# Rotary passes of an attention on Trainium2, split between two steps: two table products in the odd step, the third product and the sum in the even step behind it

## The chip, the cores and the metric

The kernel runs on one core of one Trainium2 chip. The metric is the time of one execution in device microseconds (us). TensorE, VectorE, ScalarE, GpSimd and SyncE are called PE, DVE, ACT, POOL and SP, as in the profile. Each of them works through its own instruction stream in order, and they meet at semaphores.

## The reference, cut to what matters

A two-layer block over 8 sequences of 512 tokens with width 128, all in 32-bit floats. The first layer is a causal attention with two query heads and one shared key and value, gated by a mixture of experts (8 experts, 2 per token). The second layer is a recurrent block with a gated feed-forward part. The change touches only the rotary embedding of queries and keys in the first layer:

```python
k = apply_rope(x @ Wk.T)
v = x @ Wv.T
q = jnp.einsum('btd,hkd->bhtk', x, Wq)
q = apply_rope(q)
scores = jnp.einsum('bhtk,bsk->bhts', q, k) * scale
...
# apply_rope: xr = x.reshape(..., d // 2, 2)
out = jnp.stack([xr[..., 0] * cos - xr[..., 1] * sin, xr[..., 1] * cos + xr[..., 0] * sin], axis=-1)
```

## The kernel before, in words

The program is written out per engine, in four stages. First all 4096 tokens are normalised and turned, and the router's logits are made. Then comes the attention of sequences ("batches") 0 to 6, while POOL scatters the tokens by expert into DRAM (lines 474 to 503). Then 71 tiles of 128 slots go through their experts. Last is the attention of batch 7 and the recurrent layer. The order of the work within a stage is fixed by the order in which the Python code issues instructions on each engine. There is no planner.

The attention of one batch is eight steps, k = 0 to 7. A step is one tile of 128 queries of one head, and its width is the causal part of the keys: 512 columns at k = 0 and 2, 128 at 1 and 3, 384 at 4 and 6, 256 at 5 and 7 (STEPS, line 45). So the even steps are the wide ones, and the odd steps the narrow ones. In step k the engines issue, in this order:

- PE (`attend`, L733): `scores(k)` (L687 the products, L689 the mask added on top), which needs the exponential of step k-2, since the two share a bank. In odd steps `project` for the next batch comes behind it (parts 0, 1, 2 are the two queries and the key, L668, at k = 1, 3, 5; part 3 is the value times output product, L671, at k = 7). Then `turn(k-1)` (L701, four or fewer transposes), which needs exponential k-1, and `weigh(k-2)` (L720), which needs the copy of turn k-2.
- DVE (`attend`, L1154): `row_max(k)` (L1147), which needs the scores of k, and `denominator(k-1)` (L1152, a reciprocal), which needs exponential k-1. In steps 5, 6, 1 and 2 one `combine` follows (L1140, 128x128). In steps 1, 3 and 5 one pass `rope` for the next batch follows (L1116).
- ACT (`attend`, L1539): a `head0` copy in some steps, `exponent(k)` (L1513), which needs the row maximum of k, and `turned(k-1)` (L1522). At the batch's end are the two `values` copies (L1535, L1536).

One `rope` pass is four DVE instructions on 512 columns: RT1 = bank times cosines (L1125, all partitions), the two halves of RT2 = bank times sines with the partition halves crossed (L1126, L1127, 64 partitions each), and the sum RT1 + RT2 into QT (L1130). L1127 is the last to read the PSUM bank and counts `proj_free`. A wait on that count stands before L1130 (L1129). L1130 counts `qk_done`.

Parts 0 and 2 of a batch use PSUM bank 0, part 1 uses bank 1, part 3 uses both. So PE waits at L664 before it projects: parts 0 and 1 for the `values` copies of the batch before, part 2 for L1127 of part 0, and part 3 for L1127 of part 2. `scores(0)` of a batch waits for its third `qk_done` (L682).

Batch 0 is special on DVE: step 0 has the second half of the router's top-2 choice, step 1 the slot numbers, and step 5, behind the rope pass, `experts()` (L1109 to L1113, which lets SP start to load expert weights). Batch 7 has no rope pass.

Of the kernel before, what the change touches and what calls it, by code (L numbers as in the profile page):

```python
# [26 lines left out]
P = 128  # L27
# [50 lines left out]
def build(nc, t, out):  # L78
    ctx = ExitStack()
    with ctx:  # L80
# [164 lines left out]
        B = [ctx.enter_context(nc.psum_tensor(f"bank{i}", [P, 512], F32)) for i in range(8)]  # L245
# [760 lines left out]
        def _(dve):  # L1006
# [60 lines left out]
            def choose_both(half):  # L1067

                n = NT // 2
                tiles = slice(half * n, (half + 1) * n)  # L1070
                logits = by_expert(B[6 + half][:, 0:n * E])
                dve.wait_ge(a_lg, NSEQ // 2 * (half + 1))
                choose(0, logits, half)
                link(dve.scalar_tensor_tensor(out=LG2[:, tiles, :], in0=by_expert(OH[:, 0, :])[:, tiles, :],
                                              scalar=BELOW, in1=logits, op0=ALU.mult, op1=ALU.add))
                choose(1, LG2[:, tiles, :], half)
                cols = slice(half * n * E, (half + 1) * n * E)
                dve.tensor_tensor(SH[:, tiles, :], logits, TOP[:, 0, tiles, None].broadcast_to([P, n, E]), ALU.subtract)
                dve.tensor_tensor(DIF[:, tiles], TOP[:, 1, tiles], TOP[:, 0, tiles], ALU.subtract).then_inc(r_sh, 1)
                dve.tensor_tensor(MB[:, cols], OH[:, 0, cols], OH[:, 1, cols], ALU.add).then_inc(r_m, 1)  # L1080

            def slots():

                dve.wait_ge(r_cnt_out, 1)
                link(dve.tensor_reduce(SUMT, TOTS[:, :, 1:], AX.X, ALU.add))
                link(dve.tensor_scalar(REM, SUMT, (P - 1) / 2, ULP_IS_P, ALU.add, ALU.add))
                link(dve.tensor_scalar(TCN, REM, ULP_IS_P, None, ALU.subtract))
                dve.wait_ge(prep, 3)
                link(dve.tensor_tensor_scan(CTL, ONES, TCN, 0.0, ALU.mult, ALU.add))
                link(dve.tensor_tensor(TOTS[:, :, 0], CTL, TCN, ALU.subtract))  # L1090
                link(dve.tensor_tensor_scan(EXB.rearrange("p e n -> p (e n)"),
                                            CST[:, C_RESET:C_RESET + E * (NT + 1)],
                                            TOTS.rearrange("p e n -> p (e n)"), 0.0, ALU.mult, ALU.add))
                link(dve.tensor_tensor(POS, LOWER, EXB[:, :, 0:NT].rearrange("p e n -> p n e"), ALU.add))
                link(dve.tensor_tensor(PIC, POS.rearrange("p n e -> p (n e)")[:, None, :].broadcast_to([P, 2, NT * E]),
                                       OH, ALU.mult))
                link(dve.tensor_reduce(SLF.rearrange("p k n -> p (k n)"),
                                       PIC.rearrange("p k (n e) -> p (k n) e", e=E), AX.X, ALU.add))
                dve.tensor_copy(SLOT[:], SLF).then_inc(r_slot, 1)

            def gates():

                dve.wait_ge(r_exp, 1)
                link(dve.tensor_reduce(SUME, SH, AX.X, ALU.add))
                dve.reciprocal(GATE[0], SUME).then_inc(r_gate0, 1)

            def experts():

                link(dve.tensor_tensor(CM2, CTL[:, None, :].broadcast_to([P, SLOT_TILES, E]),  # L1109
                                       CST[:, C_TILE:C_TILE + SLOT_TILES, None].broadcast_to([P, SLOT_TILES, E]),  # L1110
                                       ALU.is_le))
                link(dve.tensor_reduce(TEF, CM2, AX.X, ALU.add))
                dve.tensor_scalar(TEXP[:], TEF, float(E - 1), None, ALU.min).then_inc(r_texp, 1)  # L1113


            def rope(b, u, part):  # L1116

                tab = 2 if part == 2 else 0
                m = 3 * b + part
                dve.wait_ge(proj_full, 4 * b + (part + 1))  # L1120
                if not (isinstance(m, int) and m == 0):
                    dve.wait_ge(qk_done, m)
                bank = B[part % 2]
                half = P // 2
                dve.tensor_tensor(RT1, bank[:], ROPE[:, tab, :], ALU.mult)  # L1125
                dve.tensor_tensor(RT2[0:half], bank[half:P, :], ROPE[half:P, tab + 1, :], ALU.mult)  # L1126
                dve.tensor_tensor(RT2[half:P], bank[0:half, :], ROPE[0:half, tab + 1, :], ALU.mult  # L1127
                                  ).then_inc(proj_free, 1)
                dve.wait_ge(proj_free, 4 * b + (part + 1))  # L1129
                dve.tensor_tensor(QT[u][part], RT1, RT2, ALU.add).then_inc(qk_done, 1)  # L1130

            def combine(b, c):

                k = {0: 2, 1: 3, 2: 6, 3: 7}[c]
                i, _ = STEPS[k]
                dve.wait_ge(pv_done, NS * b + (k + 1))
                dve.wait_ge(rd_done, NS * b + (k + 1))
                dve.wait_ge(o0_done, TPS * b + (c + 1))
                reg = B[6 + k % 2][:, 0:P]
                dve.scalar_tensor_tensor(out=SA[:, bass.ds(b * TPS + i, 1), :].rearrange("p a d -> p (a d)"), in0=reg,  # L1140
                                         scalar=RD[:, k:k + 1], in1=O0[c], op0=ALU.mult, op1=ALU.add
                                         ).then_inc(o_done, 1)

            def row_max(b, k):
                i, _ = STEPS[k]
                dve.wait_ge(s_full, NS * b + (k + 1))
                dve.tensor_reduce(NM[:, k:k + 1], B[2 + k % 2][:, 0:(i + 1) * P], AX.X, ALU.max,  # L1147
                                  negate=True).then_inc(max_done, 1)

            def denominator(b, k):  # L1150
                dve.wait_ge(exp_done, NS * b + (k + 1))
                dve.reciprocal(RD[:, k:k + 1], DEN[:, k:k + 1]).then_inc(rd_done, 1)  # L1152

            def attend(b, u, first=False, last=False):  # L1154
                for k in range(NS):
                    row_max(b, k)
                    if not (first and k == 0):
                        denominator(b if k else b - 1, (k - 1) % NS)
                    if isinstance(b, int) and b == 0:
                        if k == 0:  # L1160
                            choose_both(1)
                        if k == 1:
                            gates()
                            slots()
                    if k in (5, 6):
                        combine(b, k - 5)
                    if k in (1, 2) and not first:
                        combine(b - 1, k + 1)
                    if k in (1, 3, 5) and not last:
                        rope(b + 1, 1 - u, (k - 1) // 2)  # L1170
                    if isinstance(b, int) and b == 0 and k == 5:
                        experts()
                    if last:
                        if k == 6:
                            d_early_gate(0)
                            d_first_product()
                        if k == 7:
                            d_early_gate(1)
# [7 lines left out]
            dve.wait_ge(vo_done, 1)  # L1186
            dve.tensor_copy(CVO[:].rearrange("p h d -> p (h d)"), B[2][:, 0:2 * P]).then_inc(cvo_done, 1)
            rope(0, 0, 0)
            rope(0, 0, 1)
            choose_both(0)  # L1190
            rope(0, 0, 2)
            attend(0, 0, first=True)
            with dve.Fori(0, NB // 2) as i:
                attend(i * 2 + 1, 1)
                attend(i * 2 + 2, 0)
# [59 lines left out]
            def d_early_gate(b):  # L1255

                dve.wait_ge(d_th, b + 1)
                y = Y0[:, tiles(b), :]
                dve.scalar_tensor_tensor(out=y, in0=SIL[:, b, :].rearrange("p (i d) -> p i d", d=P), scalar=1.0, in1=y,
                                         op0=ALU.add, op1=ALU.mult).then_inc(d_g0, 1)  # L1260

            def d_first_product():
                dve.wait_ge(d_g0, 1)
                dve.tensor_tensor(Y0[:, 0:TPS, :], Y0[:, 0:TPS, :], SA[:, 0:TPS, :], ALU.mult).then_inc(d_sg, 1)
# [559 lines left out]
```

## Time and profile before

| | us |
|---|---|
| median of 3 runs | 585.35 (583.39 to 586.44) |
| the profiled execution, its own time | 584.18 |
| its span, first to last instruction | 582.3 |
| from scores(0) of batch 1 to the end of batch 6's eight steps | 65.48 to 169.1 |
| PE busy over the span | 546.8 |
| DVE busy over the span | 377.0 |
| ACT busy over the span | 276.7 |
| mean granted clock | 0.985 of full speed |

PE is the engine with most busy time, but its matmul ends are modelled, so a span without idle time in the record can still have short holes. The stages follow one another: the attention of batches 0 to 6 runs to about 172, the expert tiles to about 380, and the rest is batch 7 and the recurrent layer.

### The profile page before, as it was taken

To read this page: it belongs to the slowest core of one execution; us is meant where nothing else is said; L and a number is where in the kernel's file an instruction comes from. 1 tells how busy PE (TensorE), PEld (TensorE's weight loads), DVE (VectorE), ACT (ScalarE), POOL (GpSimd) and SP (SyncE) were. 2 spreads that over 40 slices of the span, in tenths; PEclk is the share of its full clock that TensorE was granted. 3 is DMA by queue.
4 is the path that set the end of the run, shared out by engine and by line. 5 is a ranking of instruction groups with operands and counts; after the bars stand their busy time and mean duration, and the time that the engine had idled before them with its cause. 6 is when DMAs were issued, how large, how long until landed. Compare 5 with 4: busy or idle time off the path is not lost. (4 is left out here: it accounts for less than half of the span.)

```text
span 582.3 us, 13385 instructions
## 1 busy us (share of the span) xinstructions
PE 546.8 (94%) x3327; PEld 401.7 (69%) x3328; DVE 377.0 (65%) x1071; ACT 276.7 (48%) x792; POOL 255.1 (44%) x385
## 2 busy tenths in 40 slices
PE   9957899999989999999999999997999999999984
PEld 4734666667669999999999999763554454454441
DVE  6968777877755655555555655566767766776521
ACT  4513465465555445555455455564553553454320
POOL 4203554665623444444444444442554654653210
PEclk9969999999999999999999999999999999999988
DMA  9920533211117887888787887190000000000000
GB/s 285 374 73 20 176 119 137 68 59 59 41 32 208 240 231 232 240 238 234 231 236 233 242 233 225 51 262 2 0 19 1 18 18 0 18 18 9 10 18 19
DMA packets 46107, 71.77 MB, mean 123 GB/s; under 512 B 6256, under 2 KB 32016, under 8 KB 45824
## 3 DMA queue, kind: packets, MB, share of 16 engines
q1 hardware_dynamic: 31536, 57.82, 33.4%
q0 software_dynamic: 4320, 8.92, 4.6%
q10 hardware_dynamic: 10224, 4.73, 2.9%
q8 instruction: 10, 0.16, 0.1%
q14 instruction: 17, 0.14, 0.1%
HBM read 54.14 MB, written 15.74 MB: 120 GB/s over the span
## 5 line engine op out<-in xcount | busy, mean ns | idle before, releaser
L1224 DVE SCALAR_TENSOR_TENSOR AR<-bank,B1T,AR 128x128 f32<-128x128 f32 x284 | 80.4, 344 | 75.6 <-ACT AR L1601 75.4
L521 POOL DMA_INDIRECT rows_y<-YO,DST x71 | 69.8, 982 | 96.7 <-DVE YO L1208 88.3
L1601 ACT ACTIVATE AR<-bank,BGT 128x128 f32<-128x128 f32 x284 | 81.0, 368 | 57.4 <-PE bank L810 57.4
L477 POOL DMA_INDIRECT slots_x<-XR,SLOT x64 | 63.2, 987 | 51.9 <-DMA slots_x<-XR,SLOT 32.0
L827 PE MATMUL bank<-W2E,AR 128*128 x568 | 75.1, 275 | 0.5 <-DVE AR L1224 0.5
L810 PE MATMUL bank<-AR,WGE 128*128 128x128 f32 x568 | 75.1, 275 | 0.3 <-ACT AR L1594 0.3
L818 PE MATMUL bank<-AR,WGE 128*128 128x128 f32 x568 | 75.0, 275 | 0.0
L827 PEld LDWEIGHTS bank<-W2E,AR 128*128 128x128 f32 x568 | 69.1, 192 | 0.7 <-issue 0.7
L810 PEld LDWEIGHTS bank<-AR,WGE 128*128 128x128 f32 x568 | 69.0, 192 | 0.6 <-issue 0.6
L818 PEld LDWEIGHTS bank<-AR,WGE 128*128 128x128 f32 x568 | 69.1, 192 | 0.0
L1513 ACT ACTIVATE AR<-bank,AR 128x512 f32<-128x512 f32 (+1 forms) x64 | 33.8, 529 | 64.9 <-DVE AR L1147 64.9
L720 PE MATMUL bank<-AR 128*128 128x128 f32 x320 | 46.7, 277 | 0.9 <-ACT AR L1531 0.9
L687 PE MATMUL bank<-AR 128*128 128x128 f32 (+3 forms) x128 | 46.2, 445 | 0.0
L1147 DVE TENSOR_REDUCE AR<-bank 128x1 f32<-128x512 f32 (+1 forms) x64 | 30.7, 483 | 23.7 <-PE bank L689 23.7
L1708 ACT ACTIVATE W1E<-bank 128x512 f32<-128x512 f32 x32 | 19.1, 597 | 56.7 <-PE bank L937 56.7
L701 PEld LDWEIGHTS bank<-CST,AR 128*128 128x128 f32 x160 | 17.6, 141 | 36.7 <-ACT AR L1513 27.9
L720 PEld LDWEIGHTS bank<-AR 128*128 128x128 f32 x320 | 40.8, 192 | 1.7 <-ACT AR L1522 1.6
L1381 DVE TENSOR_TENSOR W1E<-bank,W1E 128x512 f32<-128x512 f32 x32 | 22.1, 690 | 25.9 <-PE bank L943 24.7
L701 PE MATMUL bank<-CST,AR 128*128 128x128 f32 x160 | 29.6, 283 | 9.8 <-ACT AR L1513 9.8
L1594 ACT ACTIVATE AR<-bank 128x128 f32<-128x128 f32 x71 | 19.6, 277 | 39.6 <-PE bank L802 39.6
L948 PE MATMUL bank<-W1E,WDN 128*128 128x512 f32 x64 | 33.5, 615 | 1.5 <-DVE W1E L1381 1.3
L937 PE MATMUL bank<-WGE,WGT 128*128 128x512 f32 x64 | 33.7, 609 | 0.8 <-DVE WGE L1374 0.8
(190 smaller groups left out, 964.4 us busy)
## 6 DMA issues: line engine op xcount, KB each, us to landing
WGE<-in_wgu SPq DMA_DIRECT2D x71, 512.0 KB, 3.8
XG<-slots_x ACTq DMA_DIRECT2D x71, 65.0 KB, 3.3
slots_x<-W1E SPq DMA_DIRECT2D x7, 585.0 KB, 11.1
X<-in_x SPq DMA_DIRECT2D x8, 256.0 KB, 4.9
W2E<-in_w SPq DMA_DIRECT2D x1, 2048.0 KB, 8.7
XR<-rows_y SPq DMA_DIRECT2D x8, 256.0 KB, 4.8
XNT<-rows_y SPq DMA_DIRECT2D x8, 256.0 KB, 5.1
out<-X SPq DMA_DIRECT2D x8, 256.0 KB, 2.3
```

The costliest lines, as they stand in the source:

```text
L477: pool.indirect_dma_start(out=slots_x, out_offset=bass.IndirectOffsetOnAxis(ap=SLOT[:, k, n:n + 1], axis=0), in_=XR[:, n, :], in_offset=No ...
L521: pool.indirect_dma_start(out=rows_y, out_offset=bass.IndirectOffsetOnAxis(ap=DST[q][:, 0:1], axis=0), in_=YO[q % 2][:], in_offset=None).t ...
L687: pe.matmul(bank[:, 0:(i + 1) * P], QT[u][h][:, i * P:(i + 1) * P], QT[u][2][:, 0:(i + 1) * P], start=True, stop=False)
L701: mm = pe.transpose(B[4 + k % 2][:, j * P:(j + 1) * P], PR[k % 2][:, j * P:(j + 1) * P], ident)
L720: mm = pe.matmul(reg, PT[k % 2][:, j * P:(j + 1) * P], U[u][:, j, h * P:(h + 1) * P], start=(j == 0), stop=(j == i))
L810: mm = pe.matmul(B[1 + u][:, c * P:(c + 1) * P], WB[:, q, c * P:(c + 1) * P], XT[u], start=True, stop=True)
L818: mm = pe.matmul(B[3 + u][:, c * P:(c + 1) * P], WB[:, q, F + c * P:F + (c + 1) * P], XT[u], start=True, stop=True)
L827: mm = pe.matmul(B[5 + u][:, 0:P], HT[u][:, c, :], W2E[:, bass.ds(e, 1), c, :], start=(c == 0), stop=(c == FC - 1))
L937: pe.matmul(B[5 - 3 * (c % 2)][:], WGT[:, c * P:(c + 1) * P], H2, start=True, stop=True).then_inc(d_g, 1)
L1224: s = dve.scalar_tensor_tensor(out=HT[u][:, c, :], in0=B[3 + u][:, c * P:(c + 1) * P], scalar=B1T[:, bass.ds(e, 1), c], in1=ZB[u][:, c, :] ...
L1513: act.activation(PR[k % 2][:, 0:(i + 1) * P], B[2 + k % 2][:, 0:(i + 1) * P], ACT.Exp, bias=NM[:, k:k + 1], accum_out=DEN[:, k:k + 1]).the ...
L1601: act.activation(ZB[u][:, c, :], B[1 + u][:, c * P:(c + 1) * P], ACT.Gelu, bias=BGT[:, bass.ds(e, 1), c]).then_inc(c_gelu, 1)
```

## The change

`rope` becomes `rope_begin` and `rope_end`. In the attention's steps the first is called where `rope` was, in steps 1, 3 and 5, and the second at the same place of the next step, 2, 4 and 6. The three passes for batch 0, which run before the attention, call both parts in a row as before. No other line is touched. No instruction is added or removed.

```diff
             def rope(b, u, part):
 
+                rope_begin(b, part)
+                rope_end(b, u, part)
+
+            def rope_begin(b, part):
+
                 tab = 2 if part == 2 else 0
                 m = 3 * b + part
                 dve.wait_ge(proj_full, 4 * b + (part + 1))
...
                 half = P // 2
                 dve.tensor_tensor(RT1, bank[:], ROPE[:, tab, :], ALU.mult)
                 dve.tensor_tensor(RT2[0:half], bank[half:P, :], ROPE[half:P, tab + 1, :], ALU.mult)
+
+            def rope_end(b, u, part):
+
+                tab = 2 if part == 2 else 0
+                bank = B[part % 2]
+                half = P // 2
                 dve.tensor_tensor(RT2[half:P], bank[0:half, :], ROPE[0:half, tab + 1, :], ALU.mult
                                   ).then_inc(proj_free, 1)
                 dve.wait_ge(proj_free, 4 * b + (part + 1))
...
                     if k in (1, 2) and not first:
                         combine(b - 1, k + 1)
                     if k in (1, 3, 5) and not last:
-                        rope(b + 1, 1 - u, (k - 1) // 2)
+                        rope_begin(b + 1, (k - 1) // 2)
+                    if k in (2, 4, 6) and not last:
+                        rope_end(b + 1, 1 - u, (k - 2) // 2)
                     if isinstance(b, int) and b == 0 and k == 5:
                         experts()
```

So the first two products stay in the odd step, and the third product (which frees the bank) goes with the sum.

## Rows read from the trace of the kernel before

**Rows 1.** The page, part 1: busy us (share of the span) x instructions.

```profile
PE 546.8 (94%) x3327; PEld 401.7 (69%) x3328; DVE 377.0 (65%) x1071; ACT 276.7 (48%) x792; POOL 255.1 (44%) x385
```

**Rows 2.** Busy us by stretch: length, PE, PEld, DVE, ACT, POOL. Batches 5, 6; sum 1-6.

```profile
134.54:151.83 17.29, 16.56 (x99) 11.71 (x98) 13.59 (x32) 9.28 (x30) 10.22 (x13) 1.00 0.17 58
...
151.83:169.10 17.27, 16.61 (x101) 11.83 (x99) 13.71 (x32) 9.54 (x33) 8.08 (x10) 1.00 0.09 31
...
sum 103.62, PE 99.52 PEld 70.52 DVE 81.83 ACT 56.57 POOL 56.02; mean PE 16.59 PEld 11.75 DVE 13.64 ACT 9.43 POOL 9.34
```

**Rows 3.** Waits, 65.4 to 169.2: engine, line, whom for: us, times, longest.

```profile
DVE AR L1152 <- ACT AR L1513: 4.4, 14, 0.3
...
PE bank L701 <- ACT AR L1513: 4.1, 12, 0.5
...
PEld bank L671 <- DVE AR L1127: 0.5, 3, 0.2
```

**Rows 4.** Timeline of batch 5, PE: start us, us, engine, line ... [idle before <-releaser].

```profile
139.38 0.22 PE L689 MATMUL bank<-BFC 128*128 128x128 bf16 x1
...
142.31 0.66 PE L701 MATMUL bank<-CST,AR 128*128 128x128 f32 x4 [0.51 <-ACT AR L1513]
...
146.53 0.55 PE L701 MATMUL bank<-CST,AR 128*128 128x128 f32 x3 [0.22 <-ACT AR L1513]
...
149.23 1.99 PE L671 MATMUL bank<-CVO,AR 128*128 128x256 f32 x8
...
151.12 0.55 PE L701 MATMUL bank<-CST,AR 128*128 128x128 f32 x3
```

**Rows 5.** Timeline of batch 5, DVE.

```profile
138.73 0.69 DVE L1126 TENSOR_TENSOR AR<-bank,ROPE 64x512 f32<-64x512 f32 x1
...
140.76 0.68 DVE L1147 TENSOR_REDUCE AR<-bank 128x1 f32<-128x512 f32 x1
...
141.44 0.33 DVE L1140 SCALAR_TENSOR_TENSOR SA<-bank,AR 128x128 f32 x1
...
141.68 0.28 DVE L1147 TENSOR_REDUCE AR<-bank 128x1 f32<-128x128 f32 x1
...
142.29 0.16 DVE L1152 RECIPROCAL AR<-AR 128x1 f32<-128x1 f32 x1 [0.33 <-ACT AR L1513]
...
142.48 0.69 DVE L1125 TENSOR_TENSOR AR<-bank,ROPE 128x512 f32<-128x512 f32 x1
...
144.61 0.69 DVE L1130 TENSOR_TENSOR AR<-AR 128x512 f32<-128x512 f32 x1
...
145.22 0.55 DVE L1147 TENSOR_REDUCE AR<-bank 128x1 f32<-128x384 f32 x1
...
147.08 0.68 DVE L1125 TENSOR_TENSOR AR<-bank,ROPE 128x512 f32<-128x512 f32 x1
...
148.48 0.68 DVE L1127 TENSOR_TENSOR AR<-bank,ROPE 64x512 f32<-64x512 f32 x1
...
149.81 0.55 DVE L1147 TENSOR_REDUCE AR<-bank 128x1 f32<-128x384 f32 x1
...
150.35 0.33 DVE L1140 SCALAR_TENSOR_TENSOR SA<-bank,AR 128x128 f32 x1
```

**Rows 6.** Timeline of batch 0, steps 5 to 7, DVE and PE.

```profile
61.68 0.74 DVE L1109 TENSOR_TENSOR W1E<-W2E,CST 128x568 f32<-128x568 f32 x1
...
63.35 0.55 DVE L1147 TENSOR_REDUCE AR<-bank 128x1 f32<-128x384 f32 x1
...
64.66 0.55 PE L701 MATMUL bank<-CST,AR 128*128 128x128 f32 x3 [1.44 <-ACT AR L1513]
```

**Rows 7.** Timeline of batch 6: a sum beside POOL, and the scatter's end.

```profile
161.83 0.96 POOL L477 DMA_INDIRECT slots_x<-XR,SLOT  x1 [0.30 <-issue]
...
161.83 0.72 DVE L1130 TENSOR_TENSOR AR<-AR 128x512 f32<-128x512 f32 x1
...
164.24 0.46 POOL L507 TENSOR_TENSOR TAPW<-TAPW,CHN 128x128 f32<-128x128 f32 x1 [1.45 <-DMA slots_x<-XR,SLOT]
```

## The prediction

> **What bounds the kernel now.** The change acts only in the attention of batches 0 to 6, so I leave the page after its first part, which says that PE is busy 546.8 of 582.3 us [rows 1], and cut the attention into stretches, one a batch. Batches 1 to 6 take 103.62 us, 17.27 each; PE is busy 16.59 of that, DVE 13.64 [rows 2]. DVE has 3.6 us a batch to spare, which looks like much. The question is where the spare time lies, and what each engine waits for.
>
> The waits of PE in this stretch have one big name: turn(k-1), L701, idle for the exponential, 4.1 us in 12 times, so two holes a batch [rows 3]. The timeline shows them: 0.51 before turn(2) at 142.31 and 0.22 before turn(4) at 146.53 [rows 4]. Both have one cause. The reduction of the wide step k+1 stands on DVE behind the four rope instructions of step k: the mask of scores(2) ends at 139.38 + 0.22 = 139.60 [rows 4], but row_max(2) starts only at 140.76 [rows 5]. The exponential follows, then the turn, 1.55 after the start of the reduction (140.76 to 142.31). So the two holes together, 0.73 us a batch or 4.4 us over six batches, are what the change could give if nothing else held PE.
>
> There is a third point, and it decides this case. project(3) at 149.23 [rows 4] needs `proj_free` from L1127 of the key's pass, which ran from 148.48 for 0.68, to 149.16 [rows 5]. It started 0.07 later. In the list of waits this is a mere 0.5 us in 3 times [rows 3], so PE and DVE arrive together there, with no slack. Whoever makes PE earlier must make this L1127 earlier too.
>
> **The change, part by part.** Nothing is added or removed on any engine, and no DMA moves. What moves: L1127, its wait and L1130, past `row_max`, `denominator` and (in steps 2 and 6) `combine` of the even step. I walk one batch, batch 5, in the order of the new stream.
>
> (a) Step 2. DVE is through its second product at 138.73 + 0.69 = 139.42 [rows 5], before the mask ends at 139.60. So row_max(2) starts at 139.60 and not at 140.76, 1.16 earlier, and turn(2) could start at 139.60 + 1.55 = 141.15. PE gets there, with its hole of 0.51 closed, at 142.31 - 0.51 = 141.80. Gain for PE: 0.51.
>
> (b) Step 4. The same, with the key's predecessor in rope: row_max(4) stands behind two products and not four. The hole before turn(4), 0.22, closes too. PE would then be 0.73 ahead of before when it comes to project(3): at 148.50.
>
> (c) Step 6, the price. The key's L1127 now stands behind row_max(6), denominator(5) and combine(1). Where is it on DVE's clock? DVE in the new order has work without a break from row_max(2) on, since PE is ahead of it. From row_max(2) to this L1127 it took 148.48 - 140.76 = 7.72 us before. To that come the first pass's L1127 and L1130, which stood ahead of row_max(2): from the two rows' pitch, L1130 at 144.61 and the reduction at 145.22, L1130 costs 0.61; L1127 with its wait costs 0.71 (two products and this one take 144.61 - 142.48 = 2.13, a third each). Then row_max(6) to the end of combine(1): 150.35 + 0.33 - 149.81 = 0.87 [rows 5]. Off it come DVE's waits for the exponential before the reciprocals of steps 3 and 5, which the earlier exponentials fill: 4.4 us in all over six batches [rows 3], 0.73 a batch; and the instruction behind such a wait starts late, 0.19 after the reciprocal (142.29 to 142.48), where three instructions in a row without a wait show none: 0.1 for each of two. The sum: 7.72 + 0.71 + 0.61 + 0.87 - 0.73 - 0.2 = 8.98. L1127 starts at 139.60 + 8.98 = 148.58, and project(3) at 148.58 + 0.68 + 0.07 = 149.33, against 149.23 before. PE comes at 148.50 and waits 0.8 us. The two holes have become one, before project(3).
>
> (d) Step 7. In the old order turn(6) starts at 151.12, 1.89 after project(3). Its exponential hangs on row_max(6) at 149.81; for 384 columns the way is 1.55 less 0.13 for the shorter reduction (0.68 against 0.55) and as much for the exponential, so about 1.3, which gives 151.1: turn(6) too met its exponential with no slack, and some of the 1.89 is a wait. In the new order row_max(6) comes some 2 us earlier, so turn(6) follows project(3) directly. What is gained is between 0 and 0.2; I take 0.15, which balances the 0.10 lost at (c).
>
> (e) The sum L1130 of the key's pass ends about 149.33 + 0.7 = 150.0, and scores(0) of the next batch wants it at 151.8: cover 1.8 us, no cost. row_max(7) needs DVE at 149.9, earlier than before. Behind the moved wait between L1127 and L1130 stand L1130 and the next row_max alone; it is a wait on DVE's own product, there in both orders. SP's copies of the next input wait for project(3), which stays in place, and POOL is not passed.
>
> So a batch keeps its length: -0.05 us, six times -0.3.
>
> (f) Batch 0. In step 5 `experts()` comes between the key's two parts. It takes 63.35 - 61.68 = 1.67 [rows 6], and now stands ahead of L1127. Before, turn(6) at 64.66 waited 1.44 us for the exponential behind it [rows 6]. New: row_max(6) loses the two instructions ahead of it (1.32) and the waits of steps 3 and 5 (0.9), 63.35 - 2.2 = 61.15; then 0.87, L1127 and the start of project(3) as in (c), 62.8; then the 1.89 of project(3), less 0.15: turn(6) at 64.5. Gain 0.15; bounds: all of the 1.44, or nothing.
>
> The sum is -0.45 us, taken against the profiled execution: 584.18 goes to 583.7. The median of the runs shown is 585.35, 1.2 above that execution, so the same sum gives 584.9. Whatever the attention wins goes on to the end: the expert tiles wait for attention's last results, and the scatter is through by 164.24 [rows 7], 4.9 us before batch 6 ends at 169.10 [rows 2].
>
> **A price from the notes.** In batch 6 a sum L1130 and a scatter issue on POOL start together at 161.83; the sum takes 0.72 us, where others take 0.69, and the issue keeps its 0.96 [rows 5, 7]. So meeting POOL costs the moved sum 0.03, 18 times at most 0.5 us, and the old places met POOL as well: I take nothing. The Trainium skill, SBUF — State Buffer, section "Who interferes with whom", says that a VectorE instruction with both inputs in SBUF contends with a GpSimd instruction that reads SBUF, and that the loser blocks for the whole instruction. By that, each moved sum that meets one could wait 0.96 us, up to 17 us for 18; the trace does not agree for the scatter's issues.
>
> **The rivals.** Half a percent, 2.9 us, is about what a measurement here can tell from no change; over six batches that is 0.48 us a batch.
>
> *Faster: the two holes close and project(3) isn't held.* Then each batch loses 0.73 and the 0.15 of (d), six times 0.88 is 5.3, and batch 0 up to 1.4: 579 to 580. The scatter's margin of 4.9 would just allow it. For it speaks the list of waits, which shows only these holes, and DVE's 3.6 spare us a batch. Against it: most of that spare time lies at the batch's start, before row_max(0), where it can't serve L1127, and the sum of (c) would have to be 0.8 too long. Half of it, 0.48 a batch, is enough to be told apart. Chance 0.11.
>
> *Slower: project(3) is held longer than (c) says.* The mechanism is DVE's waits in steps 3 and 5. I take all 0.73 + 0.2 off the sum. If ACT, which has a copy between two exponentials, does not deliver earlier, they stay, and L1127 ends 0.93 later: six times 0.88 after (d), 5.3 us, 590. In between, the point where it counts is 0.48 a batch, project(3) later than 149.8 on batch 5's clock. Against it: exponential 2 and 4 come over 1 us earlier, and the waits were 0.3 us each. Chance 0.13.
>
> *Slower by the port rule:* some sums wait for POOL as above, 0.96 each; four of them, 4 us, 589. The row at 161.83 speaks against. Chance 0.01.
>
> **How the numbers follow.** The forecast, no change that can be measured, has 0.75: it needs (c) right to 0.4 us a batch, and (c) is a sum of nine row readings, with one assumption. Within it the range is 0.35 a batch, 2.1 us, each way and the scatter of the medians, about 1. To leave out no more than 2 in 10 I take 582.7 to 587.4, a little farther up, since a new wait is easier made than lost. Faster by over 0.5%: 0.11. Slower: 0.13 + 0.01 = 0.14. Same: 0.75.
>
> **What would show it.** In the changed profile: PE's idle time before L701 for the exponential nearly gone; in its place PE and its weight loads wait for L1127 before L671, some 0.8 us a batch, about 5 us in all; DVE's wait in L1152 gone but for steps 0 and 7; batches of 17.1 to 17.4 us; row_max(2) right behind its mask. The forecast is wrong if project(3) is not held (batches under 16.9), or if the key's L1127 comes more than 9.4 us after row_max(2) (batches over 17.7).

## The result, and the profile after

| | before | changed |
|---|---|---|
| median of 14 runs each, us | 585.43 (583.39 to 587.44) | 590.0 (586.12 to 592.75) |
| ratio, changed to before | | 1.0069, 95% interval 1.0045 to 1.0093 |
| the profiled execution, us | 584.18 | 586.12, the fastest of its 14 |
| length of a batch, 1 to 6 | 17.27 | 17.70 |
| first PE instruction of the expert tiles | 172.87 | 175.27 |

The change makes the kernel 0.7% slower. The forecast was 584.9 us, no change that can be measured, with 587.4 as the upper end: it is wrong. The loss has a part that the profiled executions show, 2.40 us up to the start of the expert tiles (of which 0.4 comes back by the end, so the two profiled executions are 1.9 apart), and a rest: the medians are 4.6 apart.

The same groups of rows as before the prediction, from the changed kernel. Busy time, the page's part 1 (compare [rows 1]):

```profile
PE 545.4 (93%) x3327; PEld 405.0 (69%) x3328; DVE 377.9 (65%) x1071; ACT 277.8 (48%) x792; POOL 254.1 (43%) x385
```

Busy time by stretch, batch 5 and the sum over batches 1 to 6 (length, PE, PEld, DVE, ACT, POOL; compare [rows 2]):

```profile
136.11:153.80 17.69, 16.51 (x100) 12.06 (x99) 13.67 (x32) 9.67 (x31) 10.18 (x13) 1.00 0.15 52
...
sum 106.18, PE 99.32 PEld 72.44 DVE 82.51 ACT 58.04 POOL 57.84; mean PE 16.55 PEld 12.07 DVE 13.75 ACT 9.67 POOL 9.64
```

The length grew by 2.56 us over six batches, from 103.62 to 106.18; PE's busy time did not. So PE waits more. For what, the list of waits from 65.4 to 169.2 says (compare [rows 3]; in the changed file L1125, L1126, L1127, L1130, L1147, L1152 and L1513 of before are L1130, L1131, L1138, L1141, L1158, L1163 and L1526):

```profile
PEld bank L671 <- DVE AR L1138: 7.7, 6, 1.3
...
PEld bank L701 <- ACT AR L1526: 6.7, 24, 0.4
...
PE bank L671 <- DVE AR L1138: 5.7, 6, 1.0
...
PE bank L720 <- ACT AR L1535: 1.2, 6, 0.2
...
DVE AR L1163 <- ACT AR L1526: 0.2, 1, 0.2
```

PE's idle time before the turns, 4.1 us before, is gone from the list. PEld, the weight loads, waited for the exponential at the turns 24 times for 18.2 us; 6.7 are left. DVE's wait in the reciprocal fell from 4.4 to 0.2. In their place PE waits for the key's third product, L1138, once a batch, 5.7 us in six times. A small wait for an ACT copy before `weigh` (L720) is new as well, 0.2 a batch. Together PE idles 6.9 us for 4.1 before, and that is the growth of the batches within 0.3. This is the picture that the prediction drew, "the two holes have become one, before project(3)", only bigger (0.94 in batch 5 for the 0.8 forecast). PE's timeline in batch 5 (compare [rows 4]):

```profile
143.12 0.60 PE L701 MATMUL bank<-CST,AR 128*128 128x128 f32 x4
...
147.40 0.49 PE L701 MATMUL bank<-CST,AR 128*128 128x128 f32 x3
...
151.21 1.99 PE L671 MATMUL bank<-CVO,AR 128*128 128x256 f32 x8 [0.94 <-DVE AR L1138]
...
153.04 0.49 PE L701 MATMUL bank<-CST,AR 128*128 128x128 f32 x3
```

The batch begins at 136.11, before at 134.54. From its start, turn(2) comes at 7.01 (before 7.77) and turn(4) at 11.29 (before 11.99): PE has won the 0.7 us, as forecast. (Batch 5 of before starts with a product of 1.12 us that mostly takes 1.02, so these distances are good to 0.1.) project(3) comes at 15.10 (before 14.69), after 0.94 of idle time, and turn(6) 1.83 behind it (before 1.89). DVE's timeline from row_max(2) to the key's third product says why project(3) is late (compare [rows 5]):

```profile
141.12 0.69 DVE L1158 TENSOR_REDUCE AR<-bank 128x1 f32<-128x512 f32 x1 [0.22 <-PE bank L689]
...
141.84 0.16 DVE L1163 RECIPROCAL AR<-AR 128x1 f32<-128x1 f32 x1
...
141.92 0.33 DVE L1151 SCALAR_TENSOR_TENSOR SA<-bank,AR 128x128 f32 x1
...
142.29 0.68 DVE L1138 TENSOR_TENSOR AR<-bank,ROPE 64x512 f32<-64x512 f32 x1
...
144.57 0.69 DVE L1131 TENSOR_TENSOR AR<-bank,ROPE 64x512 f32<-64x512 f32 x1
...
145.28 0.56 DVE L1158 TENSOR_REDUCE AR<-bank 128x1 f32<-128x384 f32 x1
...
145.86 0.17 DVE L1163 RECIPROCAL AR<-AR 128x1 f32<-128x1 f32 x1
...
146.06 0.68 DVE L1138 TENSOR_TENSOR AR<-bank,ROPE 64x512 f32<-64x512 f32 x1
...
148.73 0.69 DVE L1131 TENSOR_TENSOR AR<-bank,ROPE 64x512 f32<-64x512 f32 x1
...
149.44 0.56 DVE L1158 TENSOR_REDUCE AR<-bank 128x1 f32<-128x384 f32 x1
...
150.03 0.16 DVE L1163 RECIPROCAL AR<-AR 128x1 f32<-128x1 f32 x1
...
150.11 0.33 DVE L1151 SCALAR_TENSOR_TENSOR SA<-bank,AR 128x128 f32 x1
...
150.47 0.68 DVE L1138 TENSOR_TENSOR AR<-bank,ROPE 64x512 f32<-64x512 f32 x1
```

From row_max(2) at 141.12 to L1138 at 150.47 it takes 9.35 us. The prediction's sum was 8.98. The rows show where the pitch differs from before. A reduction behind the sum came 0.61 after it (144.61 to 145.22 in [rows 5]). A reduction behind the 64-partition product L1131 comes 0.71 after it (144.57 to 145.28), and the reciprocal behind that comes 0.58 later (145.28 to 145.86), where in the kernel before it came 0.47 later (149.81 to 150.28). The 64-partition product L1138 starts 0.20 behind a reciprocal (145.86 to 146.06) and 0.37 behind a combine (141.92 to 142.29), where instructions with 128 partitions started 0.07 and 0.24 behind these (the latter is 141.44 to 141.68 in [rows 5]). There are eight such places between 141.12 and 150.47: from row_max(2), (4) and (6) to the reciprocals, from L1131 to row_max(4) and (6), and to the three L1138. Each is about 0.11 longer than between 128-partition neighbours, 0.9 us in all. Not all of that is new: the two places behind L1131 only take over from L1126, which had 0.70 to its next instruction in the old order too.

The hole of batch 0 is the other thing to see. PE's timeline there, the weight product behind experts():

```profile
62.73 1.99 PE L671 MATMUL bank<-CVO,XNT 128*128 128x256 f32 x8 [2.61 <-DVE AR L1138]
```

PE idles 2.61 us before project(3), at full clock in this execution. In the kernel before, the product started with no idle time, and the hole was 1.44, before turn(6) [rows 6]:

```profile
61.27 1.95 PE L671 MATMUL bank<-CVO,XNT 128*128 128x256 f32 x8
```

### The profile page after: what moved, and what is told of

Read it like the earlier page. It is cut to its first block and busy times, and to the rows that moved or that the text cites. A ratio compares the mean times of both kernels' runs of the same rounds, so it can differ in the third digit from the quotient of the medians.

```text
span 584.3 us, 13385 instructions
## 1 busy us (share of the span) xinstructions
PE 545.4 (93%) x3327; PEld 405.0 (69%) x3328; DVE 377.9 (65%) x1071; ACT 277.8 (48%) x792; POOL 254.1 (43%) x385
## 5 line engine op out<-in xcount | busy, mean ns | idle before, releaser
L1526 ACT ACTIVATE AR<-bank,AR 128x512 f32<-128x512 f32 (+1 forms) x64 | 33.7, 527 | 59.6 <-DVE AR L1158 59.6
L720 PE MATMUL bank<-AR 128*128 128x128 f32 x320 | 48.7, 284 | 2.3 <-ACT AR L1535 1.2
L1158 DVE TENSOR_REDUCE AR<-bank 128x1 f32<-128x512 f32 (+1 forms) x64 | 31.1, 488 | 29.3 <-PE bank L689 29.1
L720 PEld LDWEIGHTS bank<-AR 128*128 128x128 f32 x320 | 41.6, 195 | 4.8 <-ACT AR L1535 2.8
L701 PEld LDWEIGHTS bank<-CST,AR 128*128 128x128 f32 x160 | 19.4, 141 | 23.1 <-ACT AR L1526 11.0
L943 PE MATMUL bank<-WGE,WUP 128*128 128x512 f32 x64 | 33.5, 606 | 0.0
```

The source lines that it names most:

```text
L720: mm = pe.matmul(reg, PT[k % 2][:, j * P:(j + 1) * P], U[u][:, j, h * P:(h + 1) * P], start=(j == 0), stop=(j == i))
L943: pe.matmul(B[6 - 3 * (c % 2)][:], WUP[:, c * P:(c + 1) * P], H2, start=True, stop=True).then_inc(d_u, 1)
```

## The experiments

Sixteen kernels ran in four groups (e1 to e4, e5 to e8, e9 to e12, e13 to e16), each group on one chip with its own runs of the kernel before, since the times of a group move together: before's median was 585.04, 593.23, 590.98 and 594.05 us in the four. So only ratios are compared across groups, and positions in a profile only where the profile has no stalls of the kind told of at e9.

**e1: the changed kernel again.** No edit.

> The changed kernel once more, for a second profile and the granted clock of each run. Theory A (all of the loss is schedule): batches of 17.7 us, +2.4 us in all at the start of the expert tiles, and the ratio to before is 1.004 to 1.005 at equal clock. Theory B (a second loss comes on top: PE's clock is granted less in many runs of the changed kernel than in runs of before): mean clocks of 0.971 to 0.981 in most runs against 0.985 and more in before, ratio 1.007 to 1.009, and the profile shows a stretch at 0.5 that the profile on hand does not have. The batches are 17.7 us in both.

Measured: 590.1 us (585.67 to 590.76), ratio 1.0058 (1.0030 to 1.0086). Batches of 17.70, as in the first profile. The times lie in two groups, four from 585.7 to 588.0 and five from 590.1 to 590.8. The profile is of the upper group. PE's weight product behind the hole of batch 0:

```profile
63.10 3.68 PE L671 MATMUL bank<-CVO,XNT 128*128 128x256 f32 x8 [2.68 <-DVE AR L1138]
```

and the stretches around it (the third number from the end is the granted clock):

```profile
62.00:64.00 2.00, 0.90 (x2) 0.79 (x3) 1.93 (x6) 1.20 (x4) 0.90 (x2) 0.80 0.51 95
...
64.00:66.00 2.00, 2.00 (x6) 1.57 (x5) 0.18 (x2) 0.56 (x2) 0.00 (x0) 0.50 1.00 382
...
66.00:68.00 2.00, 2.00 (x11) 1.41 (x11) 0.00 (x0) 0.85 (x2) 1.00 (x2) 0.85 1.03 352
```

After the hole of 2.68 us the clock was granted at 0.5, the 1.2 GHz level, and the product took 3.68 us where it had taken 1.99. Batch 1 starts at 67.40, 2.07 later than in the first profile of the changed kernel (65.33). So there is a fall of the clock, as theory B has it. But the mean clock over all runs of e1 and of before was 0.980 and 0.981, not apart as theory B had it. And the fall isn't all that sets this profile apart. Its span is 4.5 us longer than the first one's (588.8 for 584.3): 2.06 up to the first expert instruction (177.33 for 175.27), 1.45 from there to L916 in the last stage (562.74 for 559.23), where the clock is at full speed in both, and about 1 behind that, where the clock falls in both and stays down longer in e1.

**e2: only the sum moved.** The third product goes from rope_end to rope_begin:

```diff
                 dve.tensor_tensor(RT2[0:half], bank[half:P, :], ROPE[half:P, tab + 1, :], ALU.mult)
+                dve.tensor_tensor(RT2[half:P], bank[0:half, :], ROPE[0:half, tab + 1, :], ALU.mult
+                                  ).then_inc(proj_free, 1)
...
             def rope_end(b, u, part):
...
-                dve.tensor_tensor(RT2[half:P], bank[0:half, :], ROPE[0:half, tab + 1, :], ALU.mult
-                                  ).then_inc(proj_free, 1)
```

> All three products in the odd step, the sum alone in the even step, so the bank is free before row_max(6). If the loss sits in the hold of project(3) behind the key's third product: that hold goes (the product is 0.9 to 1.4 us earlier), the two holes before turn(2) and turn(4) stay mostly closed, batches of 16.5 to 16.9 us, 3 to 4.5 us faster than before, 580.5 to 582.5 us. If the two-step form by itself costs (more boundaries on VectorE), batches stay at 17.2 or more and the time is that of before or above.

Measured: 578.03 us, ratio 0.9900 (0.9865 to 0.9935). Batches of 16.01 to 16.10, better than expected. Its timeline, DVE and then PE in the same batch:

```profile
108.38 0.68 DVE L1132 TENSOR_TENSOR AR<-bank,ROPE 64x512 f32<-64x512 f32 x1
...
109.09 0.56 DVE L1158 TENSOR_REDUCE AR<-bank 128x1 f32<-128x384 f32 x1
...
109.57 0.15 DVE L1163 RECIPROCAL AR<-AR 128x1 f32<-128x1 f32 x1
...
109.64 0.33 DVE L1151 SCALAR_TENSOR_TENSOR SA<-bank,AR 128x128 f32 x1
...
109.89 0.68 DVE L1141 TENSOR_TENSOR AR<-AR 128x512 f32<-128x512 f32 x1
...
109.23 1.95 PE L671 MATMUL bank<-CVO,AR 128*128 128x256 f32 x8
```

The key's third product L1132 stands at 108.38, ahead of row_max(6), and ends at 109.06, before PE has done scores(7). project(3) is not held. The two-step form by itself doesn't cost; it wins 1.2 us a batch, if the bank is freed in time. That is more than the 0.88 which the prediction took as the most there was. In e2 the record has PE busy through the whole of each batch, 16.06 us, while in the kernel before it was "busy" 16.59 us a batch with the same instructions: so some 0.5 us a batch of PE's recorded busy time (its ends are modelled) was not work, and could be won as well.

**e3: the key's pass whole.** Passes 0 and 1 split as in the change, part 2 whole in step 5:

```diff
-                    if k in (1, 3, 5) and not last:
+                    if k in (1, 3) and not last:
                         rope_begin(b + 1, (k - 1) // 2)
-                    if k in (2, 4, 6) and not last:
+                    if k in (2, 4) and not last:
                         rope_end(b + 1, 1 - u, (k - 2) // 2)
+                    if k == 5 and not last:
+                        rope(b + 1, 1 - u, 2)
```

> Passes 0 and 1 split as in the changed kernel, the key's pass (part 2) whole in step 5 as before. If the hold of project(3) is the cause: no hold, turn(6) waits a little for its exponential, batches of 16.7 to 17.0 us, 2 to 4 us faster than before. If splitting costs per boundary whatever the place, about 17.3, as before.

Measured: 581.32 us, ratio 0.9939 (0.9918 to 0.9960). Batches of 16.8 to 16.9. Only the weight loads still wait for the bank, PE itself doesn't:

```profile
PEld bank L701 <- ACT AR L1528: 8.7, 31, 0.4
...
PEld bank L671 <- DVE AR L1138: 1.5, 6, 0.3
```

**e5: one instruction put back.** The change, but with the key's third product (part 2) in step 5, before row_max(6):

```diff
+                if part == 2:
+                    dve.tensor_tensor(RT2[half:P], bank[0:half, :], ROPE[0:half, tab + 1, :], ALU.mult
+                                      ).then_inc(proj_free, 1)
...
             def rope_end(b, u, part):
...
-                dve.tensor_tensor(RT2[half:P], bank[0:half, :], ROPE[0:half, tab + 1, :], ALU.mult
-                                  ).then_inc(proj_free, 1)
+                if part != 2:
+                    dve.tensor_tensor(RT2[half:P], bank[0:half, :], ROPE[0:half, tab + 1, :], ALU.mult
+                                      ).then_inc(proj_free, 1)
```

> The changed kernel, with one instruction per batch put back: the key's third product (part 2) stays in step 5; passes 0 and 1 keep their third product in the even step. If the whole loss is the hold of project(3) behind that one product: no hold, batches of 16.7 to 16.8 us (17.69 less 0.95), project(3) of batch 0 not held either, 577 to 581 us. If the moved third products of parts 0 and 1 cost too, batches stay above 17.0.

Measured: 588.13 us, ratio 0.9916 (0.9888 to 0.9945). One instruction a batch, moved by one step, is the difference between slower (1.0058 in e1, and see e9 and e13) and 0.8% faster. In its profile project(3) had no idle time of PE before it in batch 0 and in all batches but one (0.20 us). With e2 and e3 this settles the schedule's part: its loss is the hold of project(3) behind the key's third product. The lengths of its batches can't be read, since the profile has stalls.

**e4: experts() later.** In the changed kernel, `k == 5` becomes `k == 6` in the condition before experts(), so they come behind the key's sum.

> The changed kernel with experts() moved from step 5 to step 6 of batch 0, behind the key's third product and sum. The schedule: project(3) of batch 0 starts up to 1.7 us earlier, so the hole of 2.6 us before it shrinks to about 0.9, and the time falls by 1.2 to 1.7 us against e1. If that hole is also what costs the clock in theory B, the time falls by 3 us or more against e1 and the mean clock goes back to 0.985; if the clock falls elsewhere, it stays as in e1.

Measured: 587.05 us, ratio 1.0036 (1.0018 to 1.0054); taken by the means of their runs, as all ratios between two experiments below, e4 to e1 is 0.9970 (0.9948 to 0.9994). Batch 1 starts at 63.59, against 65.33 in the first profile of the changed kernel, 1.74 earlier. The hole of batch 0 and the clock:

```profile
60.98 1.99 PE L671 MATMUL bank<-CVO,XNT 128*128 128x256 f32 x8 [0.95 <-DVE AR L1138]
```

The hole is 0.95 long and the product runs at full clock. The mean clock of e4's executions was 0.981, though, as in before and not the 0.985 of theory B. Again, later, as **e15**:

> As e4, same chip as e13: the hole of batch 0 shortened to 0.9 us instead of filled. Schedule 1.7 us under e13, and no fall of the clock behind it: 3 us under e13 with theory B, 1.7 us without it.

Measured: ratio 1.0002 (0.9969 to 1.0035), to e13 of the same group 0.9972 (0.9949 to 0.9995). Both are 1.7 to 1.8 us, the schedule's part alone, though the 3 us of theory B lie just inside both intervals.

**e6 and e11: the two products of the odd step swapped.**

```diff
-                dve.tensor_tensor(RT1, bank[:], ROPE[:, tab, :], ALU.mult)
                 dve.tensor_tensor(RT2[0:half], bank[half:P, :], ROPE[half:P, tab + 1, :], ALU.mult)
+                dve.tensor_tensor(RT1, bank[:], ROPE[:, tab, :], ALU.mult)
```

> The changed kernel with the two products of the odd step in the other order: the 64-partition one first, the 128-partition one last, right before row_max. In the changed kernel's trace a reduction behind a 64-partition product starts 0.71 us after it and the reciprocal behind that 0.58 after the reduction, where before they came at 0.61 (behind the sum) and 0.47. If the 64-partition form makes this, row_max(4) and row_max(6) start 0.1 earlier after the product and the reciprocals 0.1 more, a batch is 0.1 to 0.3 us shorter, 0.5 to 2 us in all. If it is the fresh order itself (any product before a reduction), the gaps of 0.71 and 0.58 stay and so does the time.

> As e6, on the chip of e9. In e6's trace the gaps around the reduction went back to 0.61 and 0.47, and the gaps ahead of the 64-partition product stood at 0.19 and 0.37. Net per batch 0.1 us: batches of 17.5 to 17.6 us, 0.5 to 1 us under e9. If e6's ratio of 1.0008 was the kernel and not its chip, it is 3 us or more under e9.

Measured: ratios 1.0008 (0.9980 to 1.0037) and 1.0011 (0.9991 to 1.0031); e11 to e9 of the same group 0.9961 (0.9943 to 0.9979). The faster rival of e11's expectation ("3 us or more") is not reached with 2.3 us, nor is it the 0.5 to 1 us of the other. DVE's timeline of e6 (L1130 is now the 64-partition product, L1131 the one on 128):

```profile
114.05 0.15 DVE L1163 RECIPROCAL AR<-AR 128x1 f32<-128x1 f32 x1
...
114.24 0.69 DVE L1130 TENSOR_TENSOR AR<-bank,ROPE 64x512 f32<-64x512 f32 x1
...
114.94 0.69 DVE L1131 TENSOR_TENSOR AR<-bank,ROPE 128x512 f32<-128x512 f32 x1
...
115.55 0.55 DVE L1158 TENSOR_REDUCE AR<-bank 128x1 f32<-128x384 f32 x1
...
116.02 0.15 DVE L1163 RECIPROCAL AR<-AR 128x1 f32<-128x1 f32 x1
```

The reduction comes 0.61 behind the 128-partition product and the reciprocal 0.47 behind that, as they did in the old order. The 64-partition product starts 0.19 behind its reciprocal. So these gaps go with the 64-partition products, as expected. In an undisturbed batch of e11, row_max(2) to L1138 took 9.22 us (108.17 to 117.39), 0.13 less than 9.35. That and an earlier project(3) in batch 0 (62.27 against 62.99 in e9) give some 1.5 of the 2.3 us.

**e7, e10 and e14: the hole of batch 0 filled.** Ten matmuls of ones, which nothing reads, ahead of project(3):

```diff
+                    if isinstance(b, int) and b == 0 and k == 7:
+                        keep_warm(4, 10)
                     if not last and k in (1, 3, 5, 7):
```

> The changed kernel with ten matmuls of ones (some 2.2 us) into a free bank put into the hole of 2.6 us before project(3) of batch 0. No dependence changes and the hole's length stays, so the schedule alone gives the time of e1. If the hole is what costs the clock in about half of the executions (e1: the weight product took 3.68 us at 0.5 of full speed behind it), the upper group of times at 590 and more goes and the median falls by 2 to 3 us against e1, to 587 to 588. If the clock falls for another reason, the times spread as in e1, median 589 to 591.

> As e7, now on the chip of e9. Theory B (the 2.6 us hole of batch 0 costs the clock in part of the executions): the upper group goes, the median is 2 to 3 us under e9's and the spread is narrower. Rival (the clock falls elsewhere, or filling costs as much elsewhere): the median is that of e9 or above it.

> As e10, same chip as e13. The profile shows the clock at full speed from 45 us on. If the fall of the clock is what the timed runs lose beyond the schedule's 2 to 2.5 us, the ratio to e13 is 0.995 to 0.998 (1 to 3 us); if it is given back later in the attention, the two agree within 0.1 per cent.

with the changed kernel beside them as **e9** and **e13**:

> The changed kernel beside e10 and e11 on one chip. Batches of 17.7 us and the weight product of batch 0 behind a hole of 2.6 us, as in e1. If the clock falls in part of the executions, the times form two groups some 3 us apart (e1: 585.7 to 588.0 and 590.1 to 590.8).

> The changed kernel beside e14 to e16 on one chip, with the hole of 2.6 us before project(3) of batch 0. Four of the five profiles so far with this hole unfilled show PE's clock at half of full speed behind it; so in this profile too, or in part of the timed runs.

Measured, as ratios to before: e7 1.0056 (1.0029 to 1.0083), e10 1.0043 (1.0016 to 1.0070), e14 1.0019 (0.9989 to 1.0049); e9 1.0059 (1.0036 to 1.0082), e13 1.0014 (0.9984 to 1.0043), where the changed kernel isn't told from before. Filled to unfilled in the same group: e10 to e9 0.9994 (0.9971 to 1.0017), e14 to e13 0.9999 (0.9975 to 1.0023). The product behind the filled hole, and the stretches, in e10:

```profile
62.98 1.99 PE L671 MATMUL bank<-CVO,XNT 128*128 128x256 f32 x8 [0.48 <-issue]
```

```profile
62.00:64.00 2.00, 1.52 (x8) 0.93 (x7) 1.93 (x5) 1.14 (x4) 0.78 (x2) 1.00 0.49 82
...
64.00:66.00 2.00, 2.00 (x13) 1.63 (x12) 0.06 (x1) 1.22 (x4) 0.00 (x0) 1.00 1.00 388
...
66.00:68.00 2.00, 2.00 (x15) 1.56 (x14) 0.88 (x3) 1.54 (x4) 1.15 (x2) 1.00 1.00 367
```

The clock stays at full speed, in all three profiles with the hole filled. In the profiles with the hole left open it fell in five of six (e1, e6, e9, e11, e13, not in the first). So the hole brings the clock down, and batch 1 starts 1 to 2.5 us later for it (65.4 to 65.7 in the three filled profiles, 66.6 to 68.1 in the five). But the time doesn't follow: by the interval, filling wins 1.7 us at most in e10 and loses 1.0 at most. In e9 and e10 this advantage was down to 0.31 us when batch 5 started (140.84 and 140.53), and at the first expert instruction it was gone, there (180.52 and 180.83) and in e13 and e14 (182.66 and 182.72). That is the other outcome which the text of e14 names, time given back later in the attention; what gives it back isn't shown. Both profiles of e9 and e10 have stalls that the first group's don't have; in e9, from 65.4 to 169.2:

```profile
ACT AR L1526 <- issue: 14.1, 16, 1.3
...
DVE AR L1158 <- issue: 5.6, 1, 5.6
```

"issue" means that the record shows nothing that the engine waits for. The four profiles of the first group have none on ACT in this stretch. What they are is not known, and they hide effects of 0.2%.

**e16: the same hole in the kernel before.** The first instruction of experts() three times:

```diff
-                link(dve.tensor_tensor(CM2, ...
+                for _ in range(3):
+                    link(dve.tensor_tensor(CM2, ...
```

> The kernel before, with the first instruction of experts() issued three times, so that VectorE is 1.5 us later once, in batch 0, and PE's hole before turn(6) there grows from 1.4 to 2.9 us. No rotary pass is split. If any hole of this length at this place costs the clock: the profile shows half speed behind it, and the time is 3 to 4 us above before. If the clock's fall belongs to the split form, the time is 1.5 us above before (1.002 to 1.003) and the clock stays.

Measured: ratio 1.0000 (0.9968 to 1.0033). The profile shows the fall:

```profile
65.58 0.90 PE L701 MATMUL bank<-CST,AR 128*128 128x128 f32 x3 [3.07 <-ACT AR L1514]
...
67.13 1.91 PE L687 MATMUL bank<-AR 128*128 128x512 f32 x2
```

```profile
64.00:66.00 2.00, 0.42 (x2) 0.42 (x3) 1.60 (x7) 1.14 (x5) 1.56 (x2) 0.90 0.10 33
...
66.00:68.00 2.00, 2.00 (x9) 1.48 (x8) 0.00 (x0) 1.99 (x7) 1.39 (x3) 0.50 0.98 184
```

The hole before turn(6) is 3.07 us, and behind it the scores on 512 columns take 1.91 where they took 1.02. So the fall belongs to the hole, not to the split. And here too the time didn't follow, neither the 1.5 us of schedule nor the clock's.

**e8 and e12: going for the fastest.** e8 is e2 with experts() in step 6. e12 is e8 with the 128-partition product last of the three, where it counts the bank free.

> e2 (sum alone moved) with experts() in step 6 of batch 0, behind row_max(6) and the key's sum. turn(6) of batch 0 waits less for its exponential: up to 1.4 us less than e2 there, 576 to 578 us. If that wait is hidden by now, as e2.

> e8 with the 128-partition product last of the three, where it counts the bank free, and the sum in the even step. The reduction behind it starts 0.61 and not 0.71 after it, twice a batch, while the first 64-partition product pays the same ahead of it: 0 to 0.2 us a batch. 576 to 578.5 us, the ratio 0.985 to 0.989. If VectorE no longer binds in e8 (its list of waits has PE waiting for the exponential for 0.1 us at most), no change against e8's 0.987.

Measured: ratios 0.9870 (0.9832 to 0.9908) and 0.9901 (0.9864 to 0.9938). With e2's 0.9900 these are one result within their intervals: about 1.1% faster than before, whatever the place of experts() and the order of the products. Once the bank is free early, no effect of DVE's order shows within these intervals of 0.4%.

## Why the prediction was wrong

**What bounds the kernel: right.** The two holes before turn(2) and turn(4) came from the rope ahead of the wide reduction, and they closed. PE and DVE met without slack at project(3), and that decided the case. e2, e3 and e5 turn only that point and swing the result from a loss to a gain.

**(a), (b): right.** PE was 0.7 us ahead of before at turn(4), as forecast.

**(c): the step that failed, by its size.** "L1127 starts at 139.60 + 8.98" had 8.98 us from row_max(2); it measured 9.35. Two errors stand against each other. Around the 64-partition products the sum was 0.64 us too short (0.26 in step 2, 0.22 in step 4, 0.16 in step 6), because I took the pitch of each instruction, the time from its start to the next one's, from the old order, where its neighbours were others. And the waits that vanished gave back 1.20 us and not 0.93: from row_max(3) to RT1 the old order took 0.80 (141.68 to 142.48), the new takes 0.27 (143.62 to 143.89), and in step 5 it is 1.32 and 0.65. The net 0.37 us, six times, is 2.2 us. It lies within the 0.4 us a batch that the forecast allowed (c) for "no change", and just inside the prediction's own sign of being wrong, 9.4 us and batches over 17.7. So this step took up the allowance and left no room for anything else.

**From the profiled execution to the median: a term taken over without a reason.** The prediction added 1.2 us to its sum, since before's median lay so far above its profiled execution. For the changed kernel it is 3.9 (590.0 for 586.12). The forecast missed by 5.1 us: 2.4 of it is the schedule, +1.9 from profile to profile where -0.45 was summed, and 2.7 is this term. The schedule alone would have ended at 587.3, just inside the range.

**(d): right in sign, small.** project(3) to turn(6) shrank by 0.06, where 0.15 had been taken. With (c) that makes the batch 0.43 longer instead of 0.05 shorter (0.10 + 0.37 - 0.06, within 0.02).

**(e): right.** scores(0) never waited for the key's sum.

**(f): right in its sum, blind to the clock.** Batch 1 started 0.15 earlier, as forecast (65.33 for 65.48). But the text put L1127 behind experts() and worked out a start of project(3) at 62.8 without saying what this is for PE: a hole of 2.6 us where there was none. In five of six profiles the clock fell behind it, which put the start of batch 1 off by 1.2 to 2.7 us (66.6 to 68.1 for 65.33).

**The rivals.** The slower one named the right place, project(3) held longer than (c) says, and gave 0.48 us a batch as the point where it counts; 0.43 came. It had the wrong mechanism: DVE's waits in steps 3 and 5 did vanish (4.4 to 0.2 us). Its price, 590, was hit by the median, which is luck: it has 5.3 us of schedule where the profiles show 1.9. The port rule's rival did not come: of the 24 sums none takes over 0.73, and 0.72 was the longest in the kernel before.

**What stays open.** The medians differ by 4.6 us in the first comparison and by 5.1, 3.2 and 1.8 in e1, e9 and e13; the schedule explains 2.0 of it (profile to profile). The rest is not explained. Time does follow the mean granted clock of an execution. In the first comparison the changed kernel took 592.1 to 592.8 us at 0.971 and 0.972, and 586.1 and 587.7 at 0.985 and 0.987; in e1's group no execution of the kernel before is under 0.977, and at 0.985 (two executions of each) the two kernels are 1.8 us apart, close to the schedule's part. But the fall in batch 0 isn't shown to be what lowers that mean. Three fillings didn't lower the median, e16 added the hole without a loss, and e9's profile, which has the fall, was the fastest of its twelve executions. The clock also falls some 20 us before the end, in every profile but e9's, and from the first expert instruction to the end the 18 profiles take 408.6 to 412.8 us (before 409.4, changed 409.0, e1 411.5). So the scatter from one execution to the next has parts behind the attention, which the change doesn't touch, and in the groups with stalls an effect of this size can't be told.

## What to carry to other kernels

When work is moved away from in front of one consumer, list everything that the moved instructions release, and look for the release with no slack; here the sum could move and the product that frees the bank could not, and that one instruction decided between 0.8% faster and some 0.5% slower. An instruction's pitch doesn't belong to it alone: read it behind the instructions that it will follow, two back where the partitions change. And where two engines meet with no slack, a forecast of no change rests on a difference of two large sums, so its range must be wide.

## What the runs showed of the hardware

- **DVE instructions overlap their neighbours a little, but not around products that cross the partition halves.** Between instructions on 128 partitions the next starts 0.07 to 0.09 us before the recorded end of the last (the sum takes 0.69, the reduction comes 0.61 after it). Around the 64-partition products the order is strictly one after the other, with 0.01 to 0.05 between (0.71 for 0.69; 0.20 behind a reciprocal of 0.17; in e6 too, with the products swapped). The Trainium skill, VectorE: DVE Perf Modes, section "The DRAIN you can't avoid", says that the next operation does not start until the pipe is empty, and that one that is not held starts earlier; the rows show both.
- **It goes by where the partitions start, it seems, and not by the width.** The reciprocal behind row_max(2), both on 128 partitions, comes 0.72 after it (141.12 to 141.84) where it came 0.61 before, though DVE had been idle ahead of row_max(2). L1131 was the last to read SBUF and read it from partition 64 on; the reduction reads PSUM alone, and the reciprocal reads SBUF from 0. Behind e2's L1132, which reads from 0, the reciprocal comes after the usual 0.48 (109.09 to 109.57), while the reduction right behind it, which writes from 0 where L1132 wrote from 64, still comes after 0.71 (108.38 to 109.09). All these rows fit one rule: there is no overlap when an instruction reads PSUM or SBUF from another start partition than the last reader of that memory did, or writes it from another than the last writer. No run varied the starts by themselves, so this is not tested.
- **A hole of 2.5 to 3.1 us on PE brought the clock to its 1.2 GHz level in six of seven profiles**, e16 among them, and the holes of 1.44 us (before) and 0.95 us (e4) there did not. In the five of the changed form the product behind it took 3.15 to 3.78 us instead of 1.99. A hole of 2.37 us at 52.1 in the kernel before, behind 4.5 us of filler matmuls, did not bring it down either. In the last stage it fell behind shorter holes, 1.34 and 0.84 us with 1.2 between them (in the kernel before, 558.3 to 561.7). So the length alone doesn't decide.
